# The end of a two-part graph network: statistics of the last layer norm before the next masked sums, the last normalisation on two engines, the last store in two halves

## The chip, the cores and the metric

One core of a Trainium2 chip runs the whole program. Its engines are TensorE (PE in the profile, with its weight loads as PEld), VectorE (DVE), ScalarE (ACT), GpSimd (POOL) and SyncE (SP), which here only issues transfers. Each runs its own list of instructions in order and waits on semaphores that others raise. The metric is the device time of one execution in microseconds; of several runs the median is given.

## The reference, cut to what matters

The input is 64 graphs of 128 nodes with 128 features, an adjacency matrix for each, and a node mask.

```
x = layernorm(x + L0(x, adj, ...))            # five small graph convolutions on 25 nodes, fused
h = x
for l in range(5):                            # L1: gated graph network
    m   = einsum('bnd,de->bne', h, weight[l])
    agg = einsum('bij,bid->bjd', adj != 0, m)
    h   = gru_cell(agg, h, w_ih, w_hh, b_ih, b_hh)
x = layernorm(x + h * mask[..., None])        # over the 128 features of a node
```

Only the last line is touched by the change, and of it only the part that is worked off at the very end of the program.

## The kernel before

The 64 graphs go in visits of four (`SB = 4`), 16 visits numbered 0 to 15, and four visits are in flight at a time (`SLOTS = 4`). One layer of one visit is a window, `COLS = 512` columns wide; there are 80 windows (`WINDOWS`), 0 to 79. In a window PE multiplies the state and the aggregated neighbours with the gate weights (lines 1200 to 1202, three passes a product), ACT takes the sigmoids and the tanh (L656, L670, L672), DVE combines them (L965, L968), POOL subtracts the candidate from the old state (L470, the tile `dg`), and DVE finishes the new state `hT` in `end_step` (L864, L866). `end_step` of a window stands one window later in DVE's list. Windows 76 to 79 are the last layer of visits 12 to 15.

What leaves the network takes this path, a visit at a time:

1. PE transposes `hT` back into a PSUM bank (L1187, four 128x128 tiles).
2. DVE `leave(visit)`: masked sum with `xn`, four instructions on L873. It raises `sum_ok`.
3. DVE `norm2(visit)`: the statistics, four `bn_stats` on L881 and four `bn_aggr` on L885. It raises `ln2_st`.
4. POOL `deviation2(visit)`: from variance and mean to scale and shift, four small instructions (L429, L430, the power on L432, L434). It raises `ln2_rs`.
5. ACT `norm2(visit)`: scales the four graphs in place, four instructions on L573. It raises `ln2_ok`.
6. SP `leave(visit)`: stores the visit, 256 KB, on SP's queue (L335).

For visits 0 to 11 these steps are spread over windows of the following chunk by the tables in `Plan`. Visits 12 to 15 have no following chunk: their steps stand where the code writes them, at each engine's end. `leave(12)` and `leave(13)` on DVE still stand inside windows 78 and 79; everything else of these visits comes behind window 79. The order there is written out by hand, no scheduler moves it. Bank `PT` is used for the transposes of windows 77 and 78, so PE turns window 78's state only when `sum_ok` says that `leave(13)` has read the bank.

Of the kernel before, what the change touches and what calls it, by code (L numbers as in the profile page):

```python
# [4 lines left out]
B, N, D = 64, 128, 128  # L5
# [13 lines left out]
CHUNKS = B // CB  # L19
SB = 4  # L20
SLOTS = CB // SB
COLS = SB * N
WINDOWS = LAYERS * SLOTS * CHUNKS
# [55 lines left out]
class Plan:  # L79

    ADJ, Y, HA, HB, SA, SB, OA, OB, GATHER, BACK, REST = 2, 3, 4, 5, 6, 7, 7, 8, 9, 10, (12, 13)
# [8 lines left out]
HALVES = (range(SB // 2), range(SB // 2, SB))  # L90
# [39 lines left out]
def build(nc, x, adj, nodemask, W1, b1, W2, b2, fusion_w, weight, w_ih, w_hh, b_ih, b_hh, out):  # L130
    f32, f32r = mybir.dt.float32, mybir.dt.float32r
    ALU, ACT, AX = mybir.AluOpType, mybir.ActivationFunctionType, mybir.AxisListType
    ctx = ExitStack()
    with ctx:
# [5 lines left out]
        def sem(name):  # L140
            return ctx.enter_context(nc.semaphore(name))

        xn = sb("xn", [128, B, D])
# [63 lines left out]
        rs2, nm2 = sb("rs2", [128, SLOTS, SB]), sb("nm2", [128, SLOTS, SB])  # L207
# [8 lines left out]
                     o=(P[2], P[5]))  # L216
# [7 lines left out]
        def b1c(g, c):  # L224
# [21 lines left out]
        hi_ok, lo_ok, nat_ok, ghi_ok, glo_ok = map(sem, ("hi_ok", "lo_ok", "nat_ok", "ghi_ok", "glo_ok"))  # L246
        bn1, ln1_st, ln1_rs, ln1_ok, sum_ok, bn2, ln2_st, ln2_rs, ln2_ok, out_ok = map(sem, (
            "bn1", "ln1_st", "ln1_rs", "ln1_ok", "sum_ok", "bn2", "ln2_st", "ln2_rs", "ln2_ok", "out_ok"))
        gathered, dev1, dev2, ln1_dve, ln1_pool, hT_ok = map(sem, (
            "gathered", "dev1", "dev2", "ln1_dve", "ln1_pool", "hT_ok"))  # L250

        block = ctx.enter_context(nc.Block())

# [15 lines left out]

        def load_half(eng, dst, src, b, done):  # L270
            eng.dma_start(dst[:, b:b + CB // 2, :], src[b:b + CB // 2, :, :].rearrange("b n d -> n b d")).then_inc(done, 16)

        def load_chunk(eng, c):

# [34 lines left out]
        @block.sync  # L309
        def _(sp):  # L310

            sp.wait_ge(ac_zero, 1)
            load_adj_rows(sp, 0, SP_ADJ, ac_in[0])
            load_x_rows(sp, 0, TA, xta_in)
            load_x_rows(sp, 0, XT_SP, xt_in)
            sp.dma_start(w2[:], W2.rearrange("g (c h) d -> h g c d", c=HC)).then_inc(w2_in, 16)
            sp.wait_ge(ac_zero, 2)
            load_adj_rows(sp, 1, SP_ADJ1, ac_in[1])
            for h in range(2):
                load_half(sp, xn, x, h * CB // 2, x0_in[h])  # L320
                load_half(sp, an, adj, h * CB // 2, a0_in[h])
            sp.wait_ge(y_ps, 2)
            load_x_rows(sp, 1, range(NT), xt_in)
            for c in range(1, CHUNKS):
                if c >= 2:
                    sp.wait_ge(xa_in, 64 * (c - 1))
                load_chunk(sp, c)
                if c >= 2:
                    load_adj_rows(sp, c, range(NT), ac_in[c])

            def leave(visit):

                sp.wait_ge(ln2_ok, visit + 1)
                b = visit * SB
                sp.dma_start(out[b:b + SB, :, :].rearrange("b n d -> n b d"), xn[:, b:b + SB, :]).then_inc(out_ok, 16)  # L335

            for c in range(2, CHUNKS):
                sp.wait_ge(y_ps, 2 * c)
                load_x_rows(sp, c, range(NT), xt_in)
                if c == 3:  # L340
                    for slot in range(SLOTS):
                        leave(slot)
            for visit in range(SLOTS, B // SB):
                leave(visit)
            sp.wait_ge(out_ok, 16 * (B // SB))

        def counter(eng, signal):

# [9 lines left out]
        def _(pool):  # L358
# [50 lines left out]
            def gather(c):  # L409

                pool.wait_ge(oa_ok, c + 1)
                for g, done, (into, these) in gather_parts():
                    pool.wait_ge(ob_ok, (NG - 1) * c + g)
                    if done:
                        pool.wait_ge(gathered, ADDS * c + done)
                    nc.gpsimd.tensor_tensor(into, into, these, ALU.add).then_inc(gathered, 1)
# [48 lines left out]
            for w in ALL_WINDOWS:  # L465
                c = next_chunk(w)
                if c is not None and w.i == Plan.GATHER:
                    gather(c)
                pool.wait_ge(n_ok, w.k + 1)
                nc.gpsimd.tensor_tensor(dg[:, w.k % 2, :], hT[:, w.slot, :], ng[:, w.k % 2, :], ALU.subtract).then_inc(d_ok, 1)  # L470
                if w.k == 0:
                    deviation1(3)
                    norm1(3)
                    spread(1)
                if stats1(w) is not None:
                    deviation1(stats1(w))
                if stats2(w) is not None:
                    deviation2(stats2(w))
                if c is not None and w.i in Plan.ONES:
                    ones(c * SLOTS + Plan.ONES[w.i])  # L480
                if w.sg + 2 < CHUNKS and w.i == Plan.POWER:
                    power(w.sg + 2)
                if w.sg + 2 < CHUNKS and w.i == Plan.SPREAD:
                    spread(w.sg + 2)
            for visit in range((CHUNKS - 1) * SLOTS, B // SB):
                deviation2(visit)

        @block.scalar
        def _(act):
# [76 lines left out]
            def norm2(visit, some=EVERY):  # L566

                o = visit % SLOTS
                if 0 in some:
                    act.wait_ge(ln2_rs, visit + 1)  # L570
                for q in some:
                    yq = xn[:, visit * SB + q, :]
                    last = nc.scalar.activation(yq, yq, ACT.Identity, bias=nm2[:, o, q:q + 1], scale=rs2[:, o, q:q + 1])  # L573
                if SB - 1 in some:
                    last.then_inc(ln2_ok, 1)

            act.wait_ge(table_ok, 1)
# [54 lines left out]
            for w in ALL_WINDOWS:  # L632
                k, s, p = w.k, w.slot, w.k % 2
# [47 lines left out]
                if w.turn == "step":  # L681
                    act.wait_ge(h_ok, k)
                    nc.scalar.copy(hhi[:, w.prev, :], hT[:, w.prev, :]).then_inc(hi_ok, 1)
            for visit in range((CHUNKS - 1) * SLOTS, B // SB):
                norm2(visit)

        @block.vector
        def _(dve):
            link = counter(dve, dve_c)
            TT, TS, STT = nc.vector.tensor_tensor, nc.vector.tensor_scalar, nc.vector.scalar_tensor_tensor  # L690
# [185 lines left out]
            def norm2(visit):  # L876

                o = visit % SLOTS
                dve.wait_ge(sum_ok, visit + 1)
                for q in EVERY:  # L880
                    last = nc.vector.bn_stats(st2[:, o, q, :], xn[:, visit * SB + q, :])  # L881
                last.then_inc(bn2, 1)
                dve.wait_ge(bn2, visit + 1)
                for q in EVERY:
                    last = nc.vector.bn_aggr(ag2[:, o, q, :], st2[:, o, q, :])  # L885
                last.then_inc(ln2_st, 1)

            degrees(0)
            low_weights(0)
            scaled_part(TA)  # L890
# [43 lines left out]
            for w in ALL_WINDOWS:  # L934
# [45 lines left out]
                    lo_neighbours(k + 2, PG)  # L980
                if w.sg + 2 < CHUNKS and w.i == Plan.SCALED:
                    scaled(w.sg + 2)
            final = B // SB - 1
            norm2(final - 3)
            leave(final - 1, PT)
            norm2(final - 2)
            end_step(WINDOWS, SLOTS - 1)
            norm2(final - 1)
            leave(final, PL)
            norm2(final)  # L990

        @block.tensor
        def _(pe):
# [343 lines left out]
```

## Time and profile before

| what | value |
|---|---|
| median of 3 runs | 546.04 us (545.37 to 546.91) |
| span of the profiled execution, first to last instruction | 544.4 us |
| median less that span | 1.6 us |
| PE busy | 519.5 us, 95% |
| DVE busy | 437.8 us, 80% |
| ACT busy | 368.6 us, 68% |
| POOL busy | 250.2 us, 46% |
| last gate product on PE begins | 526.93 us |

The profile is one execution and lists its span; what lies around the span isn't broken down, and the table gives it as the difference from the median. A share of busy time is an average over the whole program. The stretch behind the last gate product, about 17 us, is a different program from the 527 us ahead of it, and it must be read by itself.

### The profile page before, as it was taken

How to read it: one execution, taken by the hardware profiler on the slowest of the kernel's cores; microseconds unless marked ns; L12 is line 12 of the kernel's file. 1: busy time of each engine (PE TensorE's matmuls, PEld its weight loads, DVE VectorE, ACT ScalarE, POOL GpSimd, SP SyncE). 2: the span in 40 equal slices, each digit the busy share in tenths (PEclk: the TensorE clock that was granted, in tenths of full speed). 3: DMA queues.
4: the chain of work that ended last, by engine and by line, in shares of the span. 5: the costliest groups of instructions: out<-in, count | busy, mean ns of one | idle time of the engine just before them, and what ended most of it. 6: DMA issues, size and time to landing. Idle time of an engine off the chain costs nothing.

```text
span 544.4 us, 8517 instructions
## 1 busy us (share of the span) xinstructions
PE 519.5 (95%) x2991; PEld 443.9 (82%) x2991; DVE 437.8 (80%) x965; ACT 368.6 (68%) x681; POOL 250.2 (46%) x301
## 2 busy tenths in 40 slices
PE   7998899999999999999999999999999999999970
PEld 5886788888888889888888888888888888888850
DVE  4488566689989986789988986778988998878785
ACT  2446566577786676787776676687795678777644
POOL 6659222258642254448652245446542244423235
PEclk8999899999999999999999999999999999999995
DMA  5867610000000010000000000000000000100002
GB/s 141 198 178 183 161 32 5 1 0 1 2 0 1 1 32 20 21 20 21 0 2 1 0 1 21 20 20 20 0 2 1 1 1 20 39 20 0 1 0 78
DMA packets 35564, 17.29 MB, mean 32 GB/s; under 512 B 4306, under 2 KB 35483, under 8 KB 35523
## 3 DMA queue, kind: packets, MB, share of 16 engines
q1 hardware_dynamic: 32489, 15.12, 10.5%
q10 hardware_dynamic: 2393, 1.41, 0.9%
q8 instruction: 24, 0.39, 0.3%
q0 software_dynamic: 640, 0.22, 0.3%
q14 instruction: 18, 0.14, 0.1%
HBM read 12.54 MB, written 4.19 MB: 31 GB/s over the span
## 4 chain that ended last, share of the span: by engine, by line
PE 88%; DVE 6%; ACT 2%; DMA 1%; issue 1%; ACTq 1%; POOL 1%; DVEq 0%; POOLq 0%
PE p L1200 19%; PE p L1202 19%; PE p L1201 19%; PE p L1194 13%; PE p L1187 8%; PE p L1080 3%; PE p L1054 2%; PE p L1073 1%; PE p L1063 1%; DVE hT L866 1%; PE p L998 1%; DMA zg<-in_L_gnn_weight_dram 1%; DVE cg L965 1%; PE p L1004 1%; DVE cg L968 1%
## 5 line engine op out<-in xcount | busy, mean ns | idle before, releaser
L470 POOL TENSOR_TENSOR dg<-hT,ng 128x512 f32<-128x512 f32 x80 | 125.9, 1574 | 266.2 <-ACT ng L672 266.2
L1200 PE MATMUL p<-ghi,wf 128*128 128x512 f32 x240 | 101.2, 422 | 2.0 <-DVE glo L858 1.9
L1200 PE MATMUL p<-hhi,wh 128*128 128x512 f32 x237 | 100.1, 422 | 0.0
L1202 PE MATMUL p<-ghi,wf 128*128 128x512 f32 x240 | 94.5, 394 | 0.0
L1201 PE MATMUL p<-glo,wf 128*128 128x512 f32 x240 | 93.6, 390 | 0.0
L1202 PE MATMUL p<-hhi,wh 128*128 128x512 f32 x237 | 93.3, 394 | 0.0
L1201 PE MATMUL p<-hlo,wh 128*128 128x512 f32 x237 | 92.6, 391 | 0.0
L965 DVE SCALAR_TENSOR_TENSOR cg<-p,biasc,rg 128x512 f32<-128x512 f32 x80 | 59.8, 748 | 39.0 <-ACT rg L656 38.0
L656 ACT ACTIVATE rg<-p,gb 128x512 f32<-128x512 f32 x80 | 55.4, 692 | 36.6 <-PE p L1202 30.9
L672 ACT ACTIVATE ng<-cg,biasc 128x512 f32<-128x512 f32 x80 | 57.9, 724 | 23.1 <-DVE cg L968 22.9
L1194 PEld LDWEIGHTS p<-an,nat 128*128 128x128 f32 x512 | 67.2, 192 | 7.4 <-DVE glo L858 2.2
L1194 PE MATMUL p<-an,nat 128*128 128x128 f32 x512 | 67.9, 276 | 2.0 <-DVE glo L858 2.0
L852 DVE TENSOR_TENSOR hlo<-hT,hhi 128x512 fp32r<-128x512 f32 x76 | 66.7, 878 | 1.0
L670 ACT ACTIVATE zg<-p,gb 128x512 f32<-128x512 f32 x80 | 55.0, 688 | 17.8 <-PE p L1202 17.8
L968 DVE TENSOR_TENSOR cg<-cg,p 128x512 f32<-128x512 f32 x80 | 55.0, 687 | 8.7 <-DVE cg L965 0.5
L858 DVE TENSOR_TENSOR glo<-p,ghi 128x512 fp32r<-128x512 f32 x80 | 55.2, 690 | 7.3 <-ACT ghi L623 7.2
L866 DVE TENSOR_TENSOR hT<-ng,dg 128x512 f32<-128x512 f32 x80 | 56.9, 712 | 2.8
L1187 PE MATMUL p<-ident,hT 128*128 128x128 f32 x320 | 49.0, 276 | 7.4 <-DVE hT L866 7.3
L864 DVE TENSOR_TENSOR dg<-zg,dg 128x512 f32<-128x512 f32 x80 | 55.2, 690 | 0.0
L1187 PEld LDWEIGHTS p<-ident,hT 128*128 128x128 f32 x320 | 38.6, 142 | 18.8 <-DVE hT L866 12.0
L1202 PEld LDWEIGHTS p<-ghi,wf 128*128 128x128 f32 x240 | 45.0, 188 | 10.5
L652 ACT COPY nat<-p 128x512 f32<-128x512 f32 x64 | 37.6, 588 | 22.7 <-PE p L1187 21.8
(147 smaller groups left out, 855.2 us busy)
## 6 DMA issues: line engine op xcount, KB each, us to landing
xn<-in_x_dram SPq DMA_DIRECT2D x8, 512.0 KB, 4.8
an<-in_adj_dram SPq DMA_DIRECT2D x8, 512.0 KB, 7.2
out_dram<-xn SPq DMA_DIRECT2D x16, 256.0 KB, 2.3
xt<-in_x_dram SPq DMA_DIRECT2D x16, 50.0 KB
w<-in_L_gnn_W_dram ACTq DMA_DIRECT2D x1, 640.0 KB, 6.1
w<-in_L_gnn_W_dram SPq DMA_DIRECT2D x1, 640.0 KB, 6.3
zg<-in_L_gnn_weight_dram ACTq DMA_DIRECT2D x1, 320.0 KB, 4.0
xt<-in_x_dram SPq DMA_DIRECT2D x8, 36.0 KB
```

The source lines that it names most:

```text
L470: nc.gpsimd.tensor_tensor(dg[:, w.k % 2, :], hT[:, w.slot, :], ng[:, w.k % 2, :], ALU.subtract).then_inc(d_ok, 1)
L656: nc.scalar.activation(rg[:, p, :], PR[:], ACT.Sigmoid, bias=gb[:, 0:1]).then_inc(r_ok, 1)
L672: nc.scalar.activation(ng[:, p, :], cg[:, p, :], ACT.Tanh, bias=bin_).then_inc(n_ok, 1)
L852: TT(hlo[:, m % SLOTS, :], hT[:, m % SLOTS, :] if source is None else source[:], hhi[:, m % SLOTS, :], ALU.subtract).then_inc(lo_ok, 1)
L866: TT(hT[:, s, :], ng[:, p, :], dg[:, p, :], ALU.add).then_inc(h_ok, 1)
L965: STT(cg[:, p, :], PH[:], bhn, rg[:, p, :], ALU.add, ALU.mult).then_inc(t1_ok, 1)
L968: TT(cg[:, p, :], cg[:, p, :], PI[:], ALU.add).then_inc(c_ok, 1)
L1187: last = TR(bank[:, q * 128:(q + 1) * 128], src(q), ident[:])
L1194: last = MM(bank[:, q * N:(q + 1) * N], src(q), an[:, b + q, :], start=True, stop=True)
L1200: MM(bank[:], w[:, 0, cols], xhi, start=start, stop=False)
L1201: MM(bank[:], w[:, 0, cols], xlo, start=False, stop=False)
L1202: return MM(bank[:], w[:, 1, cols], xhi, start=False, stop=stop)
```

## The change

Four edits, all at the end of the program. DVE takes the statistics of visit 12 at the end of window 78 instead of behind window 79, and those of visit 13 ahead of the masked sum of visit 14 instead of behind it. POOL takes `deviation2(12)` ahead of the subtraction of window 79. The last normalisation, of visit 15, is split: ACT scales graphs 0 and 1, DVE graphs 2 and 3. The last store goes as two halves of 128 KB, the first issued by ACT, the second by SP. Store 15 is no longer in SP's loop; SP waits for 17 landings instead of 16.

```diff
+        def store_half(eng, half):
+            b = B - SB + half * (SB // 2)
+            eng.dma_start(out[b:b + SB // 2, :, :].rearrange("b n d -> n b d"), xn[:, b:b + SB // 2, :]).then_inc(out_ok, 16)
...
-            for visit in range(SLOTS, B // SB):
+            for visit in range(SLOTS, B // SB - 1):
                 leave(visit)
-            sp.wait_ge(out_ok, 16 * (B // SB))
+            sp.wait_ge(ln2_dve, 1)
+            store_half(sp, 1)
+            sp.wait_ge(out_ok, 16 * (B // SB + 1))
...
+                if w.k == WINDOWS - 1:
+                    deviation2((CHUNKS - 1) * SLOTS)
                 pool.wait_ge(n_ok, w.k + 1)
...
-            for visit in range((CHUNKS - 1) * SLOTS, B // SB):
+            for visit in range((CHUNKS - 1) * SLOTS + 1, B // SB):
                 deviation2(visit)
...
-                if SB - 1 in some:
+                if SB - 1 in some or visit == B // SB - 1:
                     last.then_inc(ln2_ok, 1)
...
-            for visit in range((CHUNKS - 1) * SLOTS, B // SB):
+            for visit in range((CHUNKS - 1) * SLOTS, B // SB - 1):
                 norm2(visit)
+            norm2(B // SB - 1, HALVES[0])
+            act.wait_ge(ln2_ok, B // SB)
+            store_half(act, 0)
...
-            final = B // SB - 1
-            norm2(final - 3)
+                if k == WINDOWS - 2:
+                    norm2(final - 3)
+            norm2(final - 2)
             leave(final - 1, PT)
-            norm2(final - 2)
             end_step(WINDOWS, SLOTS - 1)
             norm2(final - 1)
             leave(final, PL)
             norm2(final)
+            dve.wait_ge(ln2_rs, final + 1)
+            o = final % SLOTS
+            for q in HALVES[1]:
+                yq = xn[:, final * SB + q, :]
+                last = TS(yq, yq, rs2[:, o, q:q + 1], nm2[:, o, q:q + 1], ALU.mult, ALU.add)
+            last.then_inc(ln2_dve, 1)
```

DVE's list before, from the end of window 78 to the masked sum of visit 14 (`hT` on L866 ends a step, `xn` on L873 is the masked sum, `st` and `ag` are the statistics; the square brackets name the semaphore waited for):

```order
L866 TENSOR_TENSOR hT<-ng,dg 128x512 [waits e_ok]
L873 SCALAR_TENSOR_TENSOR xn<-p,maskc,xn 128x128 [waits F_ps]
L873 SCALAR_TENSOR_TENSOR xn<-p,maskc,xn 128x128 x3
L965 SCALAR_TENSOR_TENSOR cg<-p,biasc,rg 128x512 [waits r_ok]
L968 TENSOR_TENSOR cg<-cg,p 128x512 [waits t1_ok,i_ps]
L864 TENSOR_TENSOR dg<-zg,dg 128x512 [waits d_ok]
L866 TENSOR_TENSOR hT<-ng,dg 128x512 [waits e_ok]
L881 BN_STATS st<-xn 128x6 [waits sum_ok]
L881 BN_STATS st<-xn 128x6 x3
L885 BN_AGGR ag<-st 128x2 [waits bn2]
L885 BN_AGGR ag<-st 128x2 x3
L873 SCALAR_TENSOR_TENSOR xn<-p,maskc,xn 128x128 [waits F_ps]
```

The same piece of DVE's list in the changed kernel, whose lines are numbered differently (L878 ends a step, L885 is the masked sum, L893 and L897 are the statistics, L978 and L981 combine the gates):

```order
L878 TENSOR_TENSOR hT<-ng,dg 128x512 [waits e_ok]
L893 BN_STATS st<-xn 128x6 [waits sum_ok]
L893 BN_STATS st<-xn 128x6 x3
L897 BN_AGGR ag<-st 128x2 [waits bn2]
L897 BN_AGGR ag<-st 128x2 x3
L885 SCALAR_TENSOR_TENSOR xn<-p,maskc,xn 128x128 [waits F_ps]
L885 SCALAR_TENSOR_TENSOR xn<-p,maskc,xn 128x128 x3
L978 SCALAR_TENSOR_TENSOR cg<-p,biasc,rg 128x512 [waits r_ok]
L981 TENSOR_TENSOR cg<-cg,p 128x512 [waits t1_ok,i_ps]
L876 TENSOR_TENSOR dg<-zg,dg 128x512 [waits d_ok]
L878 TENSOR_TENSOR hT<-ng,dg 128x512 [waits e_ok]
L893 BN_STATS st<-xn 128x6 [waits sum_ok]
```

One set of statistics (that of visit 12) has moved from behind window 79's step to in front of window 79's masked sum (that of visit 13); the statistics that now stand behind window 79's step are those of visit 13.

POOL's list in the changed kernel, around the last subtraction (L479, `dg`; it was L470 before, with all four small groups behind it):

```order
L436 TENSOR_SCALAR rs<-ag 128x4 [waits ln2_st]
L437 TENSOR_SCALAR nm<-ag 128x4
L439 TENSOR_TENSOR rs<-rs,minus_half 128x4 [waits dev2]
L441 TENSOR_TENSOR nm<-nm,rs 128x4 [waits dev2]
L479 TENSOR_TENSOR dg<-hT,ng 128x512 [waits n_ok]
L436 TENSOR_SCALAR rs<-ag 128x4 [waits ln2_st]
```

The first group, `deviation2(12)`, now stands ahead of the subtraction that window 79 waits for; three groups are left behind it.

## Rows read from the trace of the kernel before

**Rows 1.** Windows: length; busy us of PE, PEld, DVE, ACT, POOL; clock; DMA share; GB/s.

```profile
520.00:525.00 5.00, 4.73 (x25) 3.66 (x23) 3.86 (x8) 2.10 (x3) 1.19 (x2) 1.00 0.00 0
530.00:534.00 4.00, 0.28 (x3) 0.04 (x1) 3.90 (x20) 1.41 (x4) 3.11 (x7) 0.78 0.00 0
```

**Rows 2.** Chain of waits behind window 79: start us, us, what.

```profile
529.57 0.79 DVE st L881 x4
...
530.38 0.38 DVE ag L885 x4
530.76 1.01 DVE xn L873 x4
...
539.75 0.49 ACT xn L573
540.24 0.38 ACTq L134
540.63 0.77 ACT xn L573 x2
```

**Rows 3.** Timeline of DVE, windows 78 and 79: start, length, instruction, [idle before].

```profile
523.84 0.69 DVE L866 TENSOR_TENSOR hT<-ng,dg 128x512 f32<-128x512 f32 x1
525.28 1.13 DVE L873 SCALAR_TENSOR_TENSOR xn<-p,maskc,xn 128x128 f32<-128x128 f32 x4 [0.75 <-PE p L1187]
526.69 0.75 DVE L965 SCALAR_TENSOR_TENSOR cg<-p,biasc,rg 128x512 f32<-128x512 f32 x1 [0.29 <-ACT rg L656]
```

**Rows 4.** Timeline of POOL behind window 78.

```profile
524.03 1.64 POOL L470 TENSOR_TENSOR dg<-hT,ng 128x512 f32<-128x512 f32 x1 [3.81 <-ACT ng L672]
529.07 1.62 POOL L470 TENSOR_TENSOR dg<-hT,ng 128x512 f32<-128x512 f32 x1 [3.40 <-ACT ng L672]
530.85 0.19 POOL L429 TENSOR_SCALAR rs<-ag 128x4 f32<-128x4 f32 x1 [0.16 <-DVE ag L885]
531.27 1.01 POOL L432 TENSOR_TENSOR rs<-rs,minus_half 128x4 f32<-128x4 f32 x1
532.36 0.20 POOL L434 TENSOR_TENSOR nm<-nm,rs 128x4 f32<-128x4 f32 x1
538.00 0.19 POOL L429 TENSOR_SCALAR rs<-ag 128x4 f32<-128x4 f32 x1 [0.66 <-DVE ag L885]
```

**Rows 5.** Timeline of PE behind window 79: the transposes of the last two states.

```profile
529.62 0.66 PE L1187 MATMUL p<-ident,hT 128*128 128x128 f32 x4 [2.30 <-DVE hT L866]
534.32 1.11 PE L1187 MATMUL p<-ident,hT 128*128 128x128 f32 x4 [4.04 <-DVE hT L866]
```

**Rows 6.** Timeline of DVE and POOL: two long DVE subtractions, each beside a POOL instruction.

```profile
419.02 1.64 POOL L470 TENSOR_TENSOR dg<-hT,ng 128x512 f32<-128x512 f32 x1 [3.66 <-ACT ng L672]
419.43 1.78 DVE L852 TENSOR_TENSOR hlo<-hT,hhi 128x512 fp32r<-128x512 f32 x1
...
444.24 1.01 POOL L432 TENSOR_TENSOR rs<-rs,minus_half 128x4 f32<-128x4 f32 x1
444.31 0.67 DVE L852 TENSOR_TENSOR hlo<-hT,hhi 128x512 fp32r<-128x512 f32 x1
```

**Rows 7.** Timeline of DVE in the first layer norm: two graphs scaled on DVE.

```profile
35.58 0.65 DVE L846 TENSOR_SCALAR xn<-xn,rs,nm 128x128 f32<-128x128 f32 x2
```

**Rows 8.** Timeline of SP: issue of the last store.

```profile
541.42 0.37 SPq L335 DMA_DIRECT2D out_dram<-xn  x1
```

**Rows 9.** DMA issues: the last store; loads on ACT's queue (KB, us to landing).

```profile
out_dram<-xn SPq DMA_DIRECT2D x1, 256.0 KB, 2.5
...
w<-in_L_gnn_W_dram ACTq DMA_DIRECT2D x1, 640.0 KB, 6.1
...
rg<-in_L_gnn_w_ih_dram ACTq DMA_DIRECT2D x1, 192.0 KB, 2.6
```

**Rows 10.** Windows behind the last issue: the packets of the last store.

```profile
542.30:542.50 0.20, 0.00 (x0) 0.00 (x0) 0.00 (x0) 0.00 (x0) 0.00 (x0) 0.50 0.82 233
...
543.10:543.30 0.20, 0.00 (x0) 0.00 (x0) 0.00 (x0) 0.00 (x0) 0.00 (x0) 0.50 0.83 236
```

More of the change, by code:

```diff
@@ L248, in build @@
             "bn1", "ln1_st", "ln1_rs", "ln1_ok", "sum_ok", "bn2", "ln2_st", "ln2_rs", "ln2_ok", "out_ok"))
-        gathered, dev1, dev2, ln1_dve, ln1_pool, hT_ok = map(sem, (
-            "gathered", "dev1", "dev2", "ln1_dve", "ln1_pool", "hT_ok"))
+        gathered, dev1, dev2, ln1_dve, ln1_pool, hT_ok, ln2_dve = map(sem, (
+            "gathered", "dev1", "dev2", "ln1_dve", "ln1_pool", "hT_ok", "ln2_dve"))
         block = ctx.enter_context(nc.Block())
@@ L886, in norm2 @@
                 last.then_inc(ln2_st, 1)
+            final = B // SB - 1
             degrees(0)
```

## Prediction

> **What bounds the kernel now.** I read the busy table by slices first, then the windows of its end, then the chain of waits there, then the timelines of single engines. The windows show two programs. In the 5 us from 520.00 PE is busy for 4.73; in the 4 us from 530.00 it is busy for 0.28, and DVE for 3.90 [rows 1]. So up to the last gate product PE sets the time, and this change takes nothing from PE. Behind it DVE does, and the chain shows how: from 529.57 it stays on DVE through statistics, masked sum, statistics, step, statistics, masked sum and statistics, goes through POOL's scale of visit 15 (first instruction at 538.00 [rows 4]) to the four scalings on ACT, which end at 540.63 + 0.77 = 541.40 [rows 2]. SP issues the last store at 541.42 [rows 8]; it lands 2.5 us later, at 543.92 [rows 9], and the span of 544.4 us ends 0.45 after that. Work is worth its full length there as long as DVE remains what is late.
>
> **Statistics of visit 12 out of the tail.** One set of statistics costs the chain 530.38 + 0.38 - 529.57 = 1.19 us [rows 2]. It leaves the stretch in which DVE is never idle: -1.19. It goes behind window 78's step. DVE ends that step at 524.53, then waits 0.75 us for the transposes of visit 13 and begins the masked sum at 525.28 [rows 3]. The 1.19 us cover that gap and push the masked sum back by 0.45. Behind the sum stands L965, which already waited 0.29 us for ACT's sigmoid [rows 3], so 0.16 reaches window 79's chain (tanh, subtraction, step): +0.16. If that slack is no cover, the price is the whole 0.45; if it covers more than it shows, 0.
>
> What is late next? The swap of statistics 13 and masked sum 14 keeps DVE fed while PE turns window 78's state: the transposes end at 529.62 + 0.66 = 530.28 [rows 5], 530.44 with the 0.16, and DVE asks for them at 529.57 + 0.16 + 1.19 = 530.92. The subtraction ends at 529.07 + 1.62 = 530.69 [rows 4], 530.85 with the 0.16, and DVE asks for it at 530.92 + 1.01 = 531.93. Both have half a microsecond or more to spare. The last transposes take 1.11 us behind the last step [rows 5], beside the 1.19 of statistics 14; both move together, with nearly nothing to spare in either kernel. DVE stays the bound, and the 1.03 us reach the end.
>
> **POOL's first group ahead of window 79's subtraction.** What queues behind the wait for statistics 12 is that subtraction, and DVE's last step waits for it. POOL is free from 524.03 + 1.64 = 525.67 [rows 4], the statistics end at about 525.72, and a group takes 530.85 to 532.56, 1.71 us [rows 4]. It ends near 527.4, and the subtraction before began at 529.07: 1.6 us to spare. I cost it at nothing. It also empties POOL's tail, so that visit 15 finds it free.
>
> Moving the groups earlier puts visit 13's power (L432, 1.01 us) beside DVE's last step, which reads two tiles of SBUF. The trace has both cases: beside the long subtraction on POOL a like DVE instruction took 1.78 us, beside the power it took 0.67 [rows 6], so the power did not hold DVE up. The Trainium skill (SBUF — State Buffer, section "SBUF: two separate sides") says that the port pair of VectorE and GpSimd is an exclusive lock: whichever of a GpSimd instruction and a VectorE instruction with two SBUF inputs starts first keeps the other out for its whole length. By that rule the power would hold the step; rows 6 show it for the long subtraction and not for the power. It stays a rival below.
>
> **The split normalisation.** Four scalings on ACT take 0.49 + 0.38 + 0.77 = 1.64 us, two of them 0.49 + 0.38 = 0.87 [rows 2]: -0.77. DVE's two take 0.65 for the same shapes [rows 7], start on the same semaphore and are done first; DVE has nothing else left. Were DVE's as slow as all four on ACT, the edit would give 0.
>
> **The store in two halves.** ACT would now be done at 541.40 - 1.19 + 0.16 - 0.77 = 539.60 and issue its half at 539.62; SP could issue its half 0.87 - 0.65 = 0.22 earlier, at 539.40. In the trace the first packets of the last store run 0.88 us after the issue, and five windows of 0.2 us (0.82 to 1.02 of all 16 engines' time, 233 to 289 GB/s) carry it [rows 10]: 1.0 us for 256 KB at full load. The halves then share these engines, and the bytes end 1.0 us after the first packet whichever queue they come from. The gain is the earlier start: -0.22. At best only ACT's half is left when ACT is done: 0.5 us less transfer, -0.50. The other end: no store on ACT's queue is in the trace; a load of 192 KB there landed 2.6 us after its issue, SP's 256 KB store 2.5 [rows 9]. If ACT's half takes 2.6, the term is +0.10. I take -0.22, since the share of the engines in rows 10 is the nearest row. The Trainium skill (DMA: Bandwidth & Descriptors, section "Issuing engines are not separate DMA queues") says that issuing from several engines saves only sequencer time, since all run on the same 16 engines. The full share in rows 10 fits that; by the rule alone the two queues would give nothing beyond the earlier start.
>
> **Sum.** -1.19 + 0.16 - 0.77 - 0.22 = -2.02 us. Against the profiled execution's span of 544.4 that is 542.4. The median of the runs, 546.04, stands 1.6 above the span; the change touches nothing in what lies around the span, so I move the median by the same amount: 544.0. All terms at their good ends: -1.19 + 0 - 0.77 - 0.50 = -2.46, 543.6. At their bad ends, with the split kept: -1.19 + 0.45 - 0.77 + 0.10 = -1.41, 544.6; with the split worth nothing, -0.64, 545.4.
>
> **Rivals.**
> - *The power holds the step.* Visit 13's power would run from 531.27 to 532.28 [rows 4], 0.16 later to 532.44, and DVE's step would be ready at 531.93: 0.5 us lost, -1.5, 544.5. For it: the 1.78 us [rows 6]. Against it: the 0.67.
> - *The split and the halves bring nothing.* Two queues, two semaphores and two engines at the end replace one; ACT's half lands as late as the whole did. What is left is -1.03 or less: 545.0 to 545.4. For it: ACT's queue has issued nothing since the start of the program, and the row from there is 0.1 above SP's for less data [rows 9]. Against it: the scalings are measured on both engines.
> - *The statistics only change places.* If DVE's tail is not what is late and something with the same arrival takes over, such as the last transposes, -1.19 shrinks to 0 and +0.16 stays: -0.83, 545.2. Against it: the times to spare above.
> - *Slower: the store on ACT's queue lands late.* The widest row on that queue took 6.1 us to land [rows 9], for 640 KB. A half that took this long from 539.62 would land at 545.72, and the span would end at 546.2: +1.8, 547.8. It decides from a landing time of about 4.3 us, where the gain is gone. Against it: that row carries five times the data, at a time when other loads run.
>
> **How the numbers follow.** About 0.3%, 1.6 us, is what a measurement of this kernel can tell from no change; the three runs shown lie within 0.3% of each other. Forecast -2.0: 0.62. Power: 0.06. Split and halves for nothing: 0.18. Statistics only moved: 0.08. Late store: 0.06, of which most lies between no gain and slower. The forecast clears 1.6 by only 0.4, so I count about 0.55 of its 0.62 as faster, and some 0.07 of the other cases: faster 0.62. Slower 0.04, the far end of the late store. Same: 0.34. The forecast's own range is 543.5 to 544.6. The range for 8 in 10 adds the cases to -0.6 on one side and half a microsecond of difference between runs on the other: 543.0 to 545.6.
>
> **What would show it.** In the profile after: statistics at about 524.5 and no idle time of 0.75 ahead of the masked sum of visit 13; window 79's L965 about 0.16 later; POOL's group between the last two subtractions; DVE without idle time from window 79's step to the last statistics, these ending near 536.9 instead of 537.93; two scalings on each engine behind POOL; two store issues at about 539.4 and 539.6, and both landings by 541.9. A wait of DVE ahead of its last step or of the last masked sum, a step of over 0.7 us beside POOL's power, or over 2.6 us from ACT's issue to the landing would each prove a term wrong.

## The result, and the profile after

The changed kernel takes 542.51 us (median of 21 runs, 540.32 to 545.17), the kernel before 545.32 (21 runs beside them, 543.08 to 548.00). The ratio is 0.9945, 95% interval 0.993 to 0.996: 3.0 us less, 2.2 to 3.8; the two medians differ by 2.8. That is faster by more than 0.3%, as forecast, but half a microsecond below the low end of the range. Two of the three microseconds had been worked out. The rest had not, and most of this study is on it.

The profiled executions have spans of 544.37 and 539.53. Of these 4.84 us the change made only 2.34. Up to the step with which DVE ends window 78 both kernels execute the same instructions, and that step begins at 523.84 before [rows 3] and at 521.34 after: 2.50 us lie ahead of it, 2.42 of them ahead of the tanh of window 4, in what I call the start-up. The last paragraph of the experiments shows that this differs from execution to execution. So I call the stretch from that step to the end of the span the tail and compare tails: 20.53 us before, 18.19 after. (The expectation of e0 names the same step by the window whose state it finishes, 77.)

| stretch of the tail, us | before | after | predicted |
|---|---|---|---|
| step at the end of window 78 to the end of the step at the end of window 79 | 5.73 | 5.73 | +0.16 |
| to the end of the last step | 4.70 | 3.66 | -1.19 |
| to the end of the last statistics | 3.65 | 3.65 | 0 |
| to POOL's last result | 1.80 | 1.80 | 0 |
| to ACT's last scaling | 1.68 | 0.91 | -0.77 |
| to the end of the span | 2.98 | 2.44 | -0.22 |
| sum | 20.53 | 18.19 | -2.02 |
| time of a run less its span, median | 2.36 | 1.91 | 0 |

The last row is the median of 35 runs of the kernel before, those beside e0 to e3, and of the 21 of the changed kernel, three of which have 2.25 to 2.47.

The chain of waits after (start us, us, what) answers to [rows 2]:

```profile
521.34 0.69 DVE hT L878
522.03 0.80 DVE st L893 x4
...
522.85 0.38 DVE ag L897 x4
523.23 1.01 DVE xn L885 x4
524.24 0.72 DVE cg L978
...
527.07 0.79 DVE st L893 x4
...
527.88 0.38 DVE ag L897 x4
528.26 0.01 issue
528.28 1.13 DVE xn L885 x4
...
530.03 0.69 DVE hT L878
530.73 0.79 DVE st L893 x4
...
536.21 0.88 ACT xn L582 x2
```

Between two steps there is now a set of statistics each time, and one fewer behind the first of them: 527.07 to 530.73 is what was 529.57 to 534.27. DVE is without idle time from 521.34 to 534.39. ACT scales two graphs where [rows 2] show four.

The timelines of the single engines (start, length, instruction, idle before) answer to [rows 3] to [rows 8]. First DVE:

```profile
523.15 1.09 DVE L885 SCALAR_TENSOR_TENSOR xn<-p,maskc,xn 128x128 f32<-128x128 f32 x4
524.20 0.75 DVE L978 SCALAR_TENSOR_TENSOR cg<-p,biasc,rg 128x512 f32<-128x512 f32 x1
...
529.32 0.68 DVE L876 TENSOR_TENSOR dg<-zg,dg 128x512 f32<-128x512 f32 x1
...
536.21 0.60 DVE L1008 TENSOR_SCALAR xn<-xn,rs,nm 128x128 f32<-128x128 f32 x2 [1.84 <-POOL nm L441]
```

The waits of 0.75 and 0.29 us of [rows 3] are gone. Then POOL, PE, and the two queues' issues:

```profile
526.58 1.62 POOL L479 TENSOR_TENSOR dg<-hT,ng 128x512 f32<-128x512 f32 x1 [1.54 <-ACT ng L681]
...
528.78 1.01 POOL L439 TENSOR_TENSOR rs<-rs,minus_half 128x4 f32<-128x4 f32 x1
```

```profile
527.12 1.12 PE L1206 MATMUL p<-ident,hT 128*128 128x128 f32 x4 [2.29 <-DVE hT L878]
```

```profile
536.85 0.37 SPq L276 DMA_DIRECT2D out_dram<-xn  x1
...
537.12 0.42 ACTq L276 DMA_DIRECT2D out_dram<-xn  x1
```

POOL's power at 528.78 lies across DVE's step at 529.32, which takes 0.68 us all the same. PE's transposes take 1.12 us where [rows 5] had 0.66; more on that below. The DMA issues of the end (KB, us to landing):

```profile
out_dram<-xn SPq DMA_DIRECT2D x1, 128.0 KB, 1.8
out_dram<-xn ACTq DMA_DIRECT2D x1, 128.0 KB, 2.0
```

### The profile page after: what moved, and what is told of

Read it like the earlier page. It is cut to its first block, busy times and chain, and to the rows that moved or that the text cites. A ratio compares the mean times of both kernels' runs of the same rounds, so it can differ in the third digit from the quotient of the medians.

```text
span 539.5 us, 8518 instructions
## 1 busy us (share of the span) xinstructions
PE 516.7 (96%) x2991; PEld 442.2 (82%) x2991; DVE 438.0 (81%) x967; ACT 367.7 (68%) x679; POOL 249.3 (46%) x301
## 4 chain that ended last, share of the span: by engine, by line
PE 86%; DVE 7%; ACT 2%; POOL 1%; issue 1%; DMA 1%; ACTq 1%; POOLq 0%; DVEq 0%
PE p L1219 19%; PE p L1221 19%; PE p L1220 19%; PE p L1213 12%; PE p L1206 8%; PE p L1099 3%; PE p L1073 2%; PE p L1092 1%; DVE hT L878 1%; PE p L1082 1%; DVE cg L978 1%; DVE cg L981 1%; DMA zg<-in_L_gnn_weight_dram 1%; DVE dg L876 1%; PE p L1017 1%
## 5 line engine op out<-in xcount | busy, mean ns | idle before, releaser
L479 POOL TENSOR_TENSOR dg<-hT,ng 128x512 f32<-128x512 f32 x80 | 125.9, 1573 | 262.7 <-ACT ng L681 262.7
L978 DVE SCALAR_TENSOR_TENSOR cg<-p,biasc,rg 128x512 f32<-128x512 f32 x80 | 59.8, 748 | 38.7 <-ACT rg L665 37.8
L981 DVE TENSOR_TENSOR cg<-cg,p 128x512 f32<-128x512 f32 x80 | 55.0, 688 | 8.7 <-DVE cg L978 0.5
L878 DVE TENSOR_TENSOR hT<-ng,dg 128x512 f32<-128x512 f32 x80 | 56.9, 711 | 2.8
```

The source lines that it names most:

```text
L878: TT(hT[:, s, :], ng[:, p, :], dg[:, p, :], ALU.add).then_inc(h_ok, 1)
L978: STT(cg[:, p, :], PH[:], bhn, rg[:, p, :], ALU.add, ALU.mult).then_inc(t1_ok, 1)
L981: TT(cg[:, p, :], cg[:, p, :], PI[:], ALU.add).then_inc(c_ok, 1)
```

## The experiments

Each ran beside the kernel before on the same chip. The tail is from the run's own trace; "around" is the median of a run's time less its span. The expectations call the theories by letters: T, the whole effect is in the tail; S, the start-up belongs to the program; C, what lies around the span follows VectorE's list; E, it follows how the engines end; A, it follows the length of ScalarE's instruction list; L, it follows the lengths of the lists in another way. In e3 and e4 the letters A and B stand for theories of the store, which are spelled out there.

| run | tail | around | ratio (95%) |
|---|---|---|---|
| e0, before again | 20.64 | 2.33 | 1.0013 (0.9991 to 1.0034) |
| e1, statistics alone | 19.32 | 2.36 | 0.9974 (0.9951 to 0.9998) |
| e2, split alone | 19.36 | 1.90 | 0.9972 (0.9950 to 0.9994) |
| e3, one store | 18.58 | 1.88 | 0.9968 (0.9941 to 0.9994) |
| e4, halves on SP | 18.13 | 1.87 | 0.9921 (0.9891 to 0.9950) |
| e5, no swap | 18.91 | 1.89 | 0.9982 (0.9952 to 1.0011) |
| e9, halves, no DVE | 18.98 | 2.34 | 0.9986 (0.9961 to 1.0010) |
| f0, before + 4 on DVE | 20.92 | 2.34 | 0.9998 (0.9972 to 1.0024) |
| f1, after + 3 on ACT | 18.07 | 1.93 | 0.9917 (0.9892 to 0.9943) |
| f2, after + 1 on ACT | 18.08 | 2.40 | 0.9946 (0.9918 to 0.9974) |
| f3, before, DVE ends last | 20.46 | 2.31 | 0.9993 (0.9968 to 1.0018) |
| g0, before - 1 on ACT | 20.56 | 2.42 | 1.0011 (0.9986 to 1.0037) |
| h0, before, lengths of after | 20.85 | 1.91 | 1.0001 (0.9970 to 1.0032) |
| e8, shorter scale | 17.88 | 2.28 | 0.9953 (0.9930 to 0.9976) |
| g1, e8 + 8 on POOL | 17.59 | 2.20 | 0.9940 (0.9919 to 0.9961) |
| g2, after again | 18.06 | 1.91 | 0.9961 (0.9943 to 0.9979) |

The ratios scatter by the start-up (below); two profiles of one kernel agree within 0.13 in the tail (20.53 and 20.64, 18.19 and 18.06), so the parts are read from the tail and the time around the span. Kernels with the order and the ending of before lie between 20.46 and 20.92.

**e0, the kernel before once more.**

```diff
 (no edit)
```

> The kernel before, unchanged, timed against itself. The tail is counted from the start of the instruction with which VectorE ends window 77's step to the end of the span: 20.53 us in the first trace of before, 18.19 in that of after. Theory T (the whole effect is in the tail, and the time up to window 78 differs between runs of one program by a microsecond or more): ratio 1.000, tail 20.5 within 0.2, while the start of that instruction may lie anywhere between 521 and 526. Theory S (the time up to window 78 belongs to the program, and the changed one starts faster): the start lies at 523.8 within 0.3 again.

Tail 20.64 against 20.53, around 2.33 against 2.36. Two profiles of one program agree to 0.11 us in the tail, so the tail can carry differences of a few tenths, which whole spans can't.

**e1, the statistics alone.** The split and the halves are undone.

```diff
-            norm2(B // SB - 1, HALVES[0])
-            act.wait_ge(ln2_ok, B // SB)
-            store_half(act, 0)
+            (visits 12 to 15 in norm2 on ACT, one store by SP, nothing on DVE behind the statistics)
```

> Only the statistics are moved (visit 12 into window 78, visit 13 ahead of the masked sum of 14, POOL's group ahead of the last subtraction); the last normalisation and the last store are as before. Theory T: the tail is 20.53 - 1.04 = 19.5, the time about 1.0 below before. Theory S: the time is 1.5 or more below before, with the same tail. Rival (statistics and split are worth more together than apart): the tail is 20.0 or more.

**e2, the split and the halves alone.** The order of the statistics and of POOL's groups is that of before.

```diff
-                if k == WINDOWS - 2:
-                    norm2(final - 3)
-            norm2(final - 2)
+            norm2(final - 3)
             leave(final - 1, PT)
+            norm2(final - 2)
```

> Only the last normalisation and the last store are split; the statistics stand as before. Theory T: two scalings less on ACT give 0.77, the store 0.53: the tail is 20.53 - 1.30 = 19.2, the time 1.3 below before. Rival (my prediction's store term): 0.77 + 0.22, a tail of 19.5. Theory S: 2 or more below before with the same tail.

The tail falls by 1.21 in e1 and by 1.17 in e2, together 2.38, and by 2.34 with both: the parts add. (e2 holds a loss of its own of 0.13, which the next paragraph explains: its stretch up to the last step is 4.83 us.) The surprise is the other column: around the span e2 has all of the 0.45 that the changed kernel gains there, e1 none of it.

In e1 the transposes that took 1.12 us after take 0.66. The windows around them say why (length, busy us of PE, PEld, DVE, ACT, POOL, granted clock, DMA share, GB/s), after first, e1 behind it:

```profile
527.10:528.30 1.20, 1.12 (x4) 0.72 (x4) 1.15 (x9) 0.94 (x3) 1.10 (x1) 0.50 0.00 0
```

```profile
527.70:528.50 0.80, 0.66 (x4) 0.42 (x4) 0.80 (x5) 0.80 (x3) 0.80 (x1) 1.00 0.00 0
```

The granted clock is 0.50 in the one and 1.00 in the other, 1.2 and 2.4 GHz, behind the same idle time of PE (2.29 us after, 2.30 in e1). At the low level the transposes end at 528.24, and the masked sum begins at 528.28, 0.40 us behind the start of L897. In g2, where they take 0.66, it begins 0.29 behind it. In the chain the sum counts 1.13 us instead of 1.01. Nine other traces with this order, g2 of the same program among them, found the full clock and 3.53 or 3.54 us in this stretch instead of 3.66. With the order of before, too, three profiles (e2, f0, h0) have the low level and 4.82 or 4.83 instead of 4.70.

**e5, no swap.** The masked sum of visit 14 stands ahead of the statistics of visit 13 again.

```diff
-            norm2(final - 2)
             leave(final - 1, PT)
+            norm2(final - 2)
```

> The changed kernel with the masked sum of visit 14 ahead of the statistics of visit 13 again (the statistics of visit 12 stay in window 78). VectorE then waits for the transposes of window 78's state with nothing to do: 0.66 us at the full clock, 1.12 at half of it, and the statistics come behind. Theory T: the tail is 18.19 + 0.6 to 1.2 = 18.8 to 19.4. Rival (the swap is idle, only the move into window 78 counts): 18.2.

```profile
528.15 1.13 DVE L885 SCALAR_TENSOR_TENSOR xn<-p,maskc,xn 128x128 f32<-128x128 f32 x4 [0.75 <-PE p L1206]
```

On DVE's timeline the wait for the transposes is back, 0.75 us, and the stretch takes 4.37 instead of 3.53: 0.84 of the 1.17 us that the new order can bring hang on the swap. With only the first set of statistics moved, 0.33 us of the gain are left in this stretch; the rest goes into the wait on PE.

**e3, one store of 256 KB; e4, both halves on SP's queue.**

```diff
 e3
-            store_half(sp, 1)
+            leave(B // SB - 1)
-            act.wait_ge(ln2_ok, B // SB)
-            store_half(act, 0)
 e4
+            sp.wait_ge(ln2_ok, B // SB)
+            store_half(sp, 0)
-            act.wait_ge(ln2_ok, B // SB)
-            store_half(act, 0)
```

> The changed kernel with one store of 256 KB from SP behind both scalings instead of two halves. Store theory A (only the earlier start of SP's half counts, 0.22 to 0.27): tail 18.19 + 0.25 = 18.4. Store theory B (a store of 128 KB is confirmed sooner behind its last byte than one of 256 KB): tail 18.19 + 0.5 = 18.7. The last store of before landed 2.5 us after its issue where 2.3 is the median of its 16: if that 0.2 belongs to the last store, it shows here again, if it is chance, the store lands after 2.3.

> The changed kernel with both halves of the last store issued by SyncE, VectorE's half first. The second issue then waits for the first one's 0.37 us: it comes at 537.22 instead of 537.12 by the clock of the changed kernel's trace. Theory A (the 16 engines are the limit, the queue does not matter): tail 18.2 within 0.1. Rival (two queues run beside each other, one does not): the second half lands 2.3 us or more behind its issue, tail 18.5 or more. A store from SyncE has its first packet 0.91 us behind the issue, the one from ScalarE 1.02: by that the tail could even be 0.1 shorter.

One store costs the tail 0.52 us against g2 (18.58 against 18.06) and 0.39 against the profile after, which holds 0.13 of the low clock. Halves on one queue cost less than a tenth: from ACT's last scaling to the end of the span it is 2.51 us in e4, and 2.44 or 2.45 in the six traces of this ending with two queues. The second half is issued 0.18 us behind ACT's last scaling in e4 and 0.03 behind it in the profile after; it lands 1.92 us after its issue on SP and 2.00 on ACT.

**e9, halves without DVE's part.** ACT scales all four graphs and SP stores each half as it is ready.

```diff
-            act.wait_ge(ln2_ok, B // SB)
-            store_half(act, 0)
+            norm2(B // SB - 1, HALVES[1])
-            (DVE's two scalings)
```

> The changed kernel without VectorE's part: ScalarE scales all four graphs of visit 15, SyncE stores graphs 0 and 1 as soon as they are done and graphs 2 and 3 at the end. Theory T: the scaling costs 0.77 more, the last half alone is on the engines and lands 1.8 us behind its issue instead of 2.0: tail 18.19 + 0.77 - 0.2 = 18.8. Rival (a store's landing does not depend on its size): 2.3 us, tail 19.3. Time less span, by theory E (VectorE ends early) and by theory A (ScalarE's list is as long as in before): 2.36.

The tail is 18.98, 0.34 less than e1 with its one store. The second half lands 2.15 us after its issue, the first 1.81. In the kernels whose last store is slow an 8 KB packet of the queue that the trace calls "instruction" (below, a fetch) stands among the store's packets or right behind them. In before it stands in the last 3.4 us of the span (queue: packets, MB, share of 16 engines):

```profile
q1 hardware_dynamic: 528, 0.26, 26.6%
q14 instruction: 1, 0.01, 1.0%
```

It begins at 542.3, 0.9 us behind the issue, as the store's own packets do, and the last of these is through 2.20 us after the issue. For the store ahead of it that takes 1.93. In the eight profiles that end with one store of 256 KB the others of the tail land in 2.28 or 2.29 us and the last in 2.44 to 2.78. The 2.44 is e3's, where the fetch begins latest, 2.0 us behind the issue, 0.03 behind the store's last packet. A store raises its semaphore sixteen times; in all eight the first fifteen of the last store come by 2.27 to 2.29 us, and only the last is late, the more so the longer the fetch takes: 2.45 with 0.48 us (f3), 2.78 with 0.70 (f0). In the changed kernel the fetch comes too, but at 538.8, as the last of both halves' packets ends, and no increment is late there. That the fetch is what makes the last store late is read from these times; no run moved the fetch alone, and why it costs 0.15 us right behind the packets in e3 and nothing in the changed kernel is open.

**f0 to f3, what lies around the span.** The first theory was that it follows the ending: who raises the last semaphore, and how long DVE has been done. The rival was the amount of code.

```diff
 f0, before: four DVE memsets on a tile of their own at the start
+            for i in range(4):
+                nc.vector.memset(pad[:, i:i + 1], 0.0)
 f1, after: three more one-column copies on ACT at the start; f2, after: one
+            nc.scalar.copy(pad[:], P[0][:, 0:1]).then_inc(wit_ok, 1)
 f3, before: DVE waits for ACT's last scaling, then two memsets
+            dve.wait_ge(ln2_ok, final + 1)
+            for i in range(2):
+                nc.vector.memset(pad[:, i:i + 1], 0.0)
```

> The kernel before with four one-column memsets more at the start of VectorE's list, nothing else. In all executions of before (35) and of the two kernels with the old ending of VectorE and ScalarE the time less the span was 2.3 to 2.5 us; where the last normalisation is split it was 1.9 (12 and 12 executions), and the trace shows no 8 KB instruction fetch 2.1 us behind the span any more, which before has at 546.5. Theory C (a block boundary of VectorE's code, which four instructions more move): time less span falls to 1.9 and that fetch is gone, the tail stays at 20.5. Theory E (it is the way the engines end, such as who is last): 2.36 as before, fetch still there. If the boundary is that of another engine's code: 2.36 too.

> The changed kernel with three one-column copies more in ScalarE's list near the start. Theory A (the boundary is that of ScalarE's code, which got two scalings shorter and one store longer): time less span rises from 1.9 to 2.36 and the fetch behind the span is back. Theory C (VectorE's code) and theory E (how the engines end): 1.9, no fetch behind the span. The tail stays at 18.2 in all of them.

> The changed kernel with one one-column copy more near the start of ScalarE's list, which then is as long as that of before (698 entries in the trace; the changed kernel has 697, the one with one store 696, and f1 with 700 showed 1.93 with a fetch 1.8 us behind the span). Theory A (ScalarE's code, only at just this length does its last block come too late): time less span 2.36 and a fetch 2.1 us behind the span. Theory E (how the engines end): 1.9, with or without a fetch.

> The kernel before, with VectorE waiting at its end until ScalarE has scaled the last visit, and then clearing two columns of a spare tile. VectorE so ends 3 us later, at the time at which ScalarE ends, with nothing on the path to the store. Theory E (in the kernels with 1.9 VectorE ends within 3 us of the span's end, in those with 2.36 it ends 6 us ahead of it, idle): time less span falls to 1.9, and the whole time by 0.45 against before; the tail stays at 20.5. Theory A (ScalarE's code): 2.36, unchanged.

f2 decides: one copy of one column in the first microseconds, the ending untouched, and 0.49 us come back around the span (2.40 against 1.91; six of its runs 2.30 to 2.43, one 1.89). f3 changes the ending and not the median (2.31; two of its eight runs have 1.88 and 1.90), and f0's four instructions on DVE do not change it either (2.34; one of eight has 1.88). So the two levels hold for most executions of a program and not for each. E fell. The traces show what goes with it: a last fetch, 2.1 us behind the span's end. The DMA view of the 4 us behind the span, of before, of f2, and of the changed kernel:

```profile
DMA packets 1, 0.01 MB, mean 2 GB/s; under 512 B 0, under 2 KB 0, under 8 KB 0
...
q14 instruction: 1, 0.01, 0.7%
```

```profile
q14 instruction: 1, 0.01, 0.8%
```

```profile
DMA packets 0, 0.00 MB, mean 0 GB/s; under 512 B 0, under 2 KB 0, under 8 KB 0
```

f1, with three copies instead of one, has 1.93 in spite of a fetch 1.8 us behind its span: a longer list is not simply worse, and the fetch does not settle the time alone.

**g0 and h0, the mirror.** g0 takes one instruction from ACT's list in before, which was A's claim: it leaves out the rectification of the last group of the last chunk. h0 adds two DVE memsets at the start to that and so has, on every engine, a list as long as the changed kernel's (ACT 705, DVE 1090, POOL 333, SP 123, PE 6306 instructions; before had 706 and 1088 on the first two) with the ending of before.

```diff
-                for g in range(1, NG):
+                for g in range(1, NG - (c == CHUNKS - 1)):
 h0 in addition
+            for i in range(2):
+                nc.vector.memset(pad[:, i:i + 1], 0.0)
```

> The kernel before with one ScalarE instruction fewer: the rectification of the last group (96 columns) of the last chunk is left out in the middle of the program. Its ScalarE list has 697 entries, as that of the changed kernel; its end is that of before. Theory A (the length of ScalarE's list decides whether its last 8 KB block is fetched behind the span): no fetch behind the span, time less span 1.9 instead of 2.36, tail 20.5. Rival (the new ending is needed for it): 2.36.

> The kernel before with one ScalarE instruction fewer (the rectification of the last group of the last chunk is left out, as in g0) and two one-column memsets more on VectorE: every engine's compiled list is then exactly as long as in the changed kernel (ScalarE 705, VectorE 1090, GpSimd 333, SyncE 123, TensorE 6306 instructions), while the end of the program is that of before. So far 706 on ScalarE or 1088 on VectorE went with 2.3 to 2.4 us around the span, 704 or 705 with 1090 went with 1.9. Theory L (the lengths of the lists decide): time less span 1.9, no fetch behind the span, tail 20.5. Theory E (the way the program ends decides, and f2's one copy disturbed it by chance): 2.36 and the fetch.

g0 kept its 2.42, and A fell: ACT's length alone does not do it. h0 has 1.91 (1.85 to 1.93 in all its runs), no fetch behind the span, and still the tail of before: 20.85, with 0.13 of the low clock and a last store that landed in 2.71. The 0.45 us around the span go with the lengths of the instruction lists and not with the ending. The other kernels fit: with 705 on ACT and 1090 on DVE the median is 1.89 to 1.91 (the changed kernel, g2, e2, e5, h0); with 706 and 1088, 1090 or 1092, or 705 and 1088, it is 2.31 to 2.42 (before, e0, e1, e9, f2, f3, f0, g0), whichever the ending; with 704 or 708 and 1090 it is 1.87 to 1.93 (e3, e4, f1). (Counted in the traces, which show eight fewer on each of the two.) e8 and g1, with 705 and 1093, have 2.28 and 2.20. Which of the lists decides, and at which length, stays open.

**e8 and g1, a version beyond the change.** POOL's four small instructions of visit 15 become two. DVE prepares variance + epsilon and the negative mean, POOL takes the power, DVE scales three graphs straight from mean and power, ACT one. g1 adds eight POOL memsets in a pause; g2 is the changed kernel, unedited, on the same chip.

```diff
+            TS(vpe[:], ag2[:, o, :, 1], EPS, None, ALU.add).then_inc(neg_last, 1)
+            TS(ngm[:], ag2[:, o, :, 0], -1.0, None, ALU.mult).then_inc(neg_last, 1)
+            dve.wait_ge(rs_last, 1)
+            for q in (2, 3, 1):
...
+                last = TS(yq, yq, ag2[:, o, q, 0:1], rs2[:, o, q:q + 1], ALU.subtract, ALU.mult)
 g1 in addition, on POOL
+            for i in range(8):
+                nc.gpsimd.memset(pad[:, i:i + 1], 0.0)
```

> A further step from the changed kernel: for visit 15 VectorE adds the epsilon and negates the mean, GpSimd only takes the power and one product, VectorE scales graphs 2, 3 and 1 from mean and power without waiting for the product, ScalarE graph 0. In the changed kernel from the last statistics to the end of the last scaling it takes 1.80 + 0.91 = 2.71 us. Now: an addition on VectorE (about 0.2, and 0.1 to GpSimd), the power 1.03, three scalings 0.36 + 2 x 0.26 = 0.88: 2.25. The tail is 18.19 - 0.45 = 17.7, less another 0.12 if the transposes still find the full clock; the time 0.45 below the changed kernel, 3.2 below before. Rival (the hops between the engines eat it): 18.2.

> The kernel with the short scale of visit 15, and eight one-column memsets more in a pause of GpSimd's start (it waits 7 us there). In that kernel's trace the chain to the last scaling was 0.46 shorter, as worked out, but GpSimd stood 0.38 us between its last two semaphore instructions, where the changed kernel has 0.09, and time less span was 2.28. If GpSimd's code comes late there, as ScalarE's does in before: the two instructions are 0.09 apart, tail 17.6, time less span 1.9, and the time 0.5 to 0.6 below the changed kernel. If it is another engine's code: 0.38 and 2.28 again.

> The changed kernel again, beside the others on one chip: tail 18.1 to 18.2, time less span 1.9, 2.8 below before (2.35 to 2.45 in the tail, 0.45 around the span).

```profile
537.38 1.01 POOL L502 TENSOR_TENSOR rs<-vpe,minus_half 128x4 f32<-128x4 f32 x1 [0.95 <-DVE ngm L1018]
...
538.43 0.86 DVE L1022 TENSOR_SCALAR xn<-xn,ag,rs 128x128 f32<-128x128 f32 x3 [1.05 <-POOL rs L502]
...
538.86 0.49 ACT L592 ACTIVATE xn<-xn,nm,rs 128x128 f32<-128x128 f32 x1 [0.74 <-POOL nm L505]
```

In the timeline of g1 the way from the last statistics to ACT's end takes 2.25 us; after it is 1.80 + 0.91 = 2.71. e8 has the same 2.25, but its span ended 0.3 later than the landing explains: POOL stood 0.38 us between its last two semaphore instructions, 0.09 in after. So e8 missed its tail of 17.6 to 17.7, and with 2.28 around the span it makes 20.16 in all, against 19.97 for g2: by itself it wins nothing. With the eight memsets the 0.38 was gone and the tail 17.59. Tail and around together make 19.79 for g1, so 0.2 us are won. The medians, 542.30 and 543.63 over 12 runs each, differ by more, but the intervals of their ratios overlap, and the runs do not show where the rest lies. g2 has the tail and the time around the span that were expected, but not the 2.8 us below before: it is 2.1 by the ratio (1.1 to 3.1) and 1.1 by the medians.

**The start-up.** The tanh of window 4 begins anywhere from 75.9 to 79.5 us in these eighteen profiles, and from there to the step at the end of window 78 all of them take 445.0 to 445.5. S would have the early start of the changed kernel (76.09) belong to it. But e3 (78.16) has the instructions of the changed kernel up to the last store, and f3 and g1, 79.51 and 79.07, are the latest, one made from each kernel. Two profiles of one program agree (before and e0 78.51 and 78.55, after and g2 76.09 and 75.87), which speaks for S. The medians speak against it: less tail and time around the span, the 21 runs of before leave 545.32 - 20.53 - 2.36 = 522.43 us and those of the changed kernel 542.51 - 18.19 - 1.91 = 522.41, and g2, the same program once more, 543.63 - 18.06 - 1.91 = 523.66. S fell. One lead is the granted clock: from 61.20 to 64.50 it is 0.50 in both profiles of before and 1.00 in both of the changed kernel, which have 0.50 from 8.10 to 11.30. What sets the start-up of one execution was not tried. As the later stretches vary by half a microsecond at most in these traces, it is also the likely reason why 35 runs of before spread from 543.15 to 548.01.

## Why the prediction was right, and where it was wrong

The time came out 1.5 us below the forecast of 544.0. Three steps account for it: the base (0.72), what lies around the span (0.45) and the tail (0.32).

- **The base, too high.** "So I move the median by the same amount" took 546.04, the median of three runs. The median of 21 is 545.32. The failed step is the base: a gain of 2 us was set on a median that three draws from a spread of 5 us cannot fix to better than about a microsecond. Half a microsecond was allowed for the difference between runs, but the medians of 9 to 35 runs of before in these series lie from 544.72 to 546.74, those of the changed kernel at 542.51 and 543.63. On a base of 545.32 the same sum gives 543.3 and a range of 542.3 to 544.9, which holds the 542.51.
- **"The change touches nothing in what lies around the span", false.** It fell from 2.36 to 1.91. f2 and h0 show that this goes with two DVE instructions more and one on ACT less, with either ending. The prediction never counted what the change does to the lists' lengths. The 1.6 us that it carried over were the median of three executions less the span of one; run by run 2.36 lie around the span.
- **Statistics: -1.03 forecast, -1.04 measured, by two errors that cancel.** The delay of 0.16 into window 79 did not come: with the 0.75 us wait gone the masked sum counts 1.01 in the chain, not 1.13, and L978 starts at 524.20, when its gate is there. The stretch is 5.73 us in both. Against that, the "half a microsecond or more to spare" for the transposes was gone, and the masked sum began about 0.1 us late: the sum took the 0.66 us of [rows 5] for granted, and the same rows show that transposes can take 1.11. At the full clock the edit brings 1.17.
- **The swap keeps DVE fed: right**, and worth 0.84 of it (e5). POOL's first group did lie in a pause: its power ended at 524.75, the subtraction began at 526.58.
- **The power holds the step: fell.** 0.68 us beside the power, as the 0.67 of [rows 6]. The Trainium skill's rule (SBUF — State Buffer, section "SBUF: two separate sides") that such a pair excludes each other was not seen here either.
- **The split: -0.77 forecast, 1.68 to 0.91 measured.** DVE took 0.60 where the sum had 0.65.
- **The store: the mis-sized term, -0.22 forecast, -0.54 measured** (2.98 to 2.44 behind ACT's end). An undisturbed store of 256 KB lands 2.29 us after its issue, not the 2.53 of before's last store, from which the forecast started. Counted from ACT's last scaling that is 2.31, and the halves have landed after 2.02: 0.29, near the -0.22. The other 0.24 goes with the instruction fetch that fell among the last store's packets and now falls behind them. It could be found in the trace of before: the two stores ahead of the last landed in 2.29, and one packet of q14 stood in that stretch.
- **Late store on ACT's queue, and halves for nothing: fell.** ACT's half landed 2.00 us after its issue, and in e4 one queue gives 18.13, against 18.06 on two in g2. The Trainium skill (DMA: Bandwidth & Descriptors, section "Issuing engines are not separate DMA queues") says that issuing from several engines saves only the time of the issuing; e4 agrees, its second half being issued 0.15 us later than in the profile after.

## What to carry to other kernels

Behind the last big product a kernel is a chain of small instructions, and there a prediction made from the chain, term by term, came within 0.16 us here for each stretch on the engines and within 0.32 for the store; move work into the waits of that chain, and check at each move what the freed engine asks for next, at the slower of the lengths that the trace shows for it. Before a gain of 2 us is set against a base, count the base's runs and see where they spread; compare stretches of the traces, not whole spans. A few tenths can also come from what no edit names, such as where an instruction fetch falls: change the lists' lengths alone before such a difference is put down to the edit.

## What the runs showed of the hardware that was not expected

- One copy of one column at the start of the program adds 0.49 us outside the span (f2, 2.40 against 1.91 in the median), two DVE memsets with one ACT instruction fewer take 0.45 away (h0, 1.91 against 2.36), and the ending is the same each time.
- One 8 KB instruction packet among or right behind the packets of a 256 KB store goes with a landing 0.15 to 0.5 us later (2.44 to 2.78 against 2.29), and only one of the store's sixteen semaphore increments is late.
- Half the bytes do not take half the time: 128 KB land on SP's queue in 1.81 us with no other store beside them (e9's first half), 256 KB in 2.29.
- PE's four transposes of window 78's state, behind 2.3 us of idle time, ran at either level of the clock in the same program, 0.66 us in g2 and 1.12 in the profile after.
